# Post-norm layer with streamed softmax maxima: PV bursts one key tile later, casts and row fetches moved, the maxima split and turned step by step

## Time and profile before

| | us |
|---|---|
| median of 3 runs (1063.1 to 1064.48) | 1063.52 |
| the profiled execution | 1064.13 |
| its span | 1062.3 |
| PE busy | 1026.5 (97%) |
| DVE busy | 809.5 (76%) |
| ACT busy | 665.1 (63%) |
| POOL busy | 266.2 (25%) |

### The profile page before, as it was taken

One profiled execution on the slowest core, in us unless ns is written; L12 is line 12 of the kernel. 1 busy time (PEld: TensorE's weight loads), 2 busy tenths in 40 slices (PEclk: granted clock), 3 DMA queues, 4 the chain that ended last, 5 costly groups with the idle time before them and its releaser, 6 DMA issues.

```text
span 1062.3 us, 15699 instructions
## 1 busy us (share of the span) xinstructions
PE 1026.5 (97%) x5858; PEld 536.8 (51%) x5858; DVE 809.5 (76%) x1199; ACT 665.1 (63%) x1346; POOL 266.2 (25%) x227
## 2 busy tenths in 40 slices
PE   8999999999999999999999999999999999999996
PEld 3643344433443433443444443333337888888885
DVE  4899978899779799779988899999803475662535
ACT  2368877788778788778766678888863431222221
POOL 2751030141335422246200042844100000000002
PEclk9999999999999999999999999999999999999999
DMA  5274417243142512344140446531217510402011
GB/s 200 80 196 126 106 35 213 52 97 78 52 115 75 105 56 54 82 108 105 34 78 12 116 120 150 124 121 37 93 68 193 166 40 9 111 28 52 1 39 42
DMA packets 64432, 94.87 MB, mean 89 GB/s; under 512 B 37536, under 2 KB 37920, under 8 KB 62272
## 3 DMA queue, kind: packets, MB, share of 16 engines
q1 hardware_dynamic: 63776, 93.10, 33.2%
q10 hardware_dynamic: 576, 0.72, 0.2%
HBM read 53.95 MB, written 27.00 MB: 76 GB/s over the span
## 4 chain that ended last, share of the span: by engine, by line
PE 80%; DVE 10%; ACT 6%; issue 2%; DMA 1%; SPq 0%; POOL 0%; DVEq 0%; POOLq 0%
PE PS L448 21%; PE PV L467 20%; PE PSA L537 15%; PE PS L554 5%; PE PSA L426 5%; DVE nmx L964 5%; PE PS L365 4%; ACT Bn L756 3%; PE PS L493 2%; PE PSA L493 2%; DVE nmx L960 2%; DVE nmx L957 2%; ACT Bn L765 2%; PE PV L554 2%; PE PSA L365 1%
## 5 line engine op out<-in xcount | busy, mean ns | idle before, releaser
L756 ACT ACTIVATE Bn<-PS 128x512 f32<-128x512 f32 x1146 | 548.8, 559 | 125.0 <-PE PS L448 111.1
L448 PE MATMUL PS<-Qt,Kt 50*128 50x512 f32 x1146 | 391.7, 434 | 20.0 <-ACT Bn L756 18.7
L426 PE MATMUL PSA<-Kt,Qt 48*128 48x512 f32 x1024 | 390.0, 459 | 2.2 <-DVE Kt L936 0.8
L964 DVE TENSOR_REDUCE nmx<-PSA 128x1 f32<-128x1024 f32 x256 | 312.2, 1219 | 61.0 <-PE PSA L426 59.8
L448 PEld LDWEIGHTS PS<-Qt,Kt 50*128 50x128 f32 x1146 | 184.4, 184 | 323.6 <-ACT Bn L756 312.7
L467 PE MATMUL PV<-Bn 128*32 128x512 f32 x2048 | 272.8, 605 | 0.0
L426 PEld LDWEIGHTS PSA<-Kt,Qt 48*128 48x128 f32 x1024 | 174.6, 183 | 21.7 <-DVE nmx L964 6.2
L960 DVE TENSOR_REDUCE nmx<-PSA 128x1 f32<-128x512 f32 x256 | 174.5, 682 | 1.4 <-PE PSA L426 1.1
L957 DVE TENSOR_REDUCE nmx<-PSA 128x1 f32<-128x512 f32 x256 | 174.3, 681 | 0.0
L537 PE MATMUL PSA<-x1Th,wr 128*128 128x512 f32 x344 | 135.0, 393 | 0.8 <-DVE sg L1052 0.5
L537 PE MATMUL PSA<-x1Tl,wr 128*128 128x512 f32 x344 | 134.7, 392 | 0.0
(11 more groups left out here) (166 smaller groups left out, 919.4 us busy)
## 6 DMA issues: line engine op xcount, KB each, us to landing
Qt<-pscr SPq DMA_DIRECT2D x90, 128.0 KB, 4.9
A<-in_wf SPq DMA_DIRECT2D x11, 768.0 KB, 6.3
wr<-A SPq DMA_DIRECT2D x33, 256.0 KB, 2.9
pscr<-A SPq DMA_DIRECT2D x16, 512.0 KB, 3.7
vscr<-Bn SPq DMA_DIRECT2D x32, 256.0 KB, 2.0
Kt<-pscr SPq DMA_DIRECT2D x90, 64.0 KB, 2.3
A<-A SPq DMA_DIRECT2D x16, 256.0 KB, 3.7
Bn<-vscr SPq DMA_DIRECT2D x8, 512.0 KB
```

The source lines that it names most:

```text
L426: op = e.matmul(PSA[:, 2 * s + h, :], Qt[n % 3][p:p + NC_, g % 2, 128 * qt:128 * qt + 128], Kt[n % 3][p:p + NC_, 512 * h:512 * h + 512], s ...
L448: e.matmul(PS2[:, i, cols], Kt[n % 3][rows, 128 * kt:128 * kt + 128], Qt[n % 3][rows, g % 2, 512 * qh + cols.start:512 * qh + cols.stop], ...
L756: e.activation(Pb[c % NP_][:, cols], PS2[:, score_bank[c, p], cols], ACT.Exp, scale=0.25).then_inc(*act_exp.next(piece(c, p)))
L964: e.tensor_reduce(nmx[:, hh % 2, c0:c0 + 1], slot_pair(s), AX.XY, ALU.max, negate=True).then_inc(*dve_max[s].next(k))
```

## The change

- The bursts change places: behind chunk 3 of even units, behind chunk 2 of odd ones. The cut chunk is now c % 8 == 7, chunk 3 of odd units, so the pieced burst is the one of odd units and the plain one that of even units.
- Background moves with its burst: in the same units, but behind chunk 2 and the burst, and before chunk 3. `free_banks`, ScalarE's `evacuate_raw` and VectorE's additions (`first_norm`, `add_values`, `add_rows`, now between the two halves of the second step) follow.
- The casts: h0 from 6 to 7 units behind the projection, h1 from 7 to 9, "out" from 8 to 10. For job 1: units 8, 10 and 11 in place of 7, 9 and 10.
- The rows are fetched in unit 5 in place of 3.
- `turn_max` is taken apart for all query halves but the first and the last: the join stays behind step 15, the rounding stands behind step 0 of the next half, the subtraction behind step 1, the transposition behind step 2. So it ends behind the first step of the units u % 8 == 5.
- `write_max` stands in SP's units u % 8 == 4.

```diff
         rope_end = {(0, 1): (0, "h0"), (0, 2): (0, "h1"), (0, 3): (0, "out"),
-                    (0, 4): (1, "rope"), (0, 7): (1, "h0"), (0, 9): (1, "h1"), (0, 10): (1, "out")}
+                    (0, 4): (1, "rope"), (0, 8): (1, "h0"), (0, 10): (1, "h1"), (0, 11): (1, "out")}
         for at_u, j in project_at.items():
-            u0 = 16 * at_u[0] + at_u[1] + 6
-            rope_end.update({divmod(u0, 16): (j, "h0"), divmod(u0 + 1, 16): (j, "h1"), divmod(u0 + 2, 16): (j, "out")})
+            u0 = 16 * at_u[0] + at_u[1] + 7
+            rope_end.update({divmod(u0, 16): (j, "h0"), divmod(u0 + 2, 16): (j, "h1"), divmod(u0 + 3, 16): (j, "out")})
-        gather_at = {(n, {0: 13, 6: 5}.get(n, 3)): n + 2 for n in range(NG - 2)}
+        gather_at = {(n, {0: 13}.get(n, 5)): n + 2 for n in range(NG - 2)}
+        def apart(hh):
+            return 1 <= hh < 2 * NG - 1
-            return [slice(0, 128), slice(128, 512)] if c % 8 == 3 and c < 4 * SPLIT else [slice(0, 512)]
+            return [slice(0, 128), slice(128, 512)] if c % 8 == 7 and c < 4 * SPLIT else [slice(0, 512)]
         def free_banks(u):
-            last = score_bank[4 * u + 3, len(pieces(4 * u + 3)) - 1]
+            last = score_bank[4 * u + 2, 0]
             return (last + 1) % 3, last
...
-                    if u >= 1 and g == (2, 3)[u % 2]:
+                    if u >= 1 and g == (3, 2)[u % 2]:
                         weigh(u - 1)
-                if at_u in project_at:
-                    for h, i in enumerate(free_banks(u)):
-                        project_half(project_at[at_u], h, i, (0, 1, 2, 3))
...
+                        background(u)
...
                     exponent(u, g)
+                    if g == 2 and at_u in project_at:
+                        for h, i in enumerate(free_banks(u)):
+                            evacuate_raw(project_at[at_u], h, i)
                 if u >= 1:
                     finish(u - 1)
-                if at_u in project_at:
-                    for h, i in enumerate(free_banks(u)):
-                        evacuate_raw(project_at[at_u], h, i)
...
-                if k % 16 == 15:
-                    turn_max(hh)
+                if 1 in halves and k % 16 == 15:
+                    join_max(hh)
+                    if not apart(hh):
+                        high_max(hh)
+                        lower_max(hh)
+                        turn_max(hh)
+                if 1 in halves and k > 16 and k % 16 < 3 and apart(hh - 1):
+                    (high_max, lower_max, turn_max)[k % 16](hh - 1)
...
                 maximum(next(steps))
-                maximum(next(steps))
-                if at_u in norm_at:
-                    first_norm(False, 0, norm_at[at_u])
...
+                k = next(steps)
+                if at_u in norm_at or at_u in out_at or at_u == values_at:
+                    maximum(k, (0,))
...
+                    maximum(k, (1,))
+                else:
+                    maximum(k)
...
-                if steps_done(u) // 16 > steps_done(u - 1) // 16:
+                if u % 8 == 4:
                     write_max(steps_done(u) // 16 - 1)
+                if u == SPLIT - 1:
+                    write_max(2 * NG - 1)
```

More of the change, by code:

```diff
@@ L665, in tensor, with background @@
                     project_half(1, 1, 3, ((0, 1), (2, 3))[k - 2])
+            def background(u):
+                at_u, pair = divmod(u, 16), free_banks(u)
+                if at_u in project_at:
+                    for h, i in enumerate(pair):
+                        project_half(project_at[at_u], h, i, (0, 1, 2, 3))
+                if at_u == values_at:
+                    for t in range(8):
+                        value_rows(1, t, pair[t // 4])
+                if at_u in out_at:
+                    t2 = out_at[at_u]
+                    out_project(False, 0, t2, [bank(i) for i in pair], [bank_free[i] for i in pair])
+                    for j, i in enumerate(pair):
+                        bank_free[i] = dve_y.at((False, 0, 2 * t2 + j))
             for u in range(SPLIT):
@@ L945, in add_values, with maximum @@
                     ALU.add).then_inc(*dve_val.next((b, h)))
-            def maximum(k):
+            def maximum(k, halves=(0, 1)):
                 if k >= len(stream):
@@ L955, in maximum @@
                 if by_halves(k):
[L956 to L961, removed]
+                    for h in halves:
+                        w.wait_ge(*pe_max.at((k, 0) if h == 0 else k))
+                        col = nmx[:, hh % 2, c0 + 16 * (h == 0):c0 + 16 * (h == 0) + 1]
+                        e.tensor_reduce(col, slot_pair(s)[:, h, :], AX.X, ALU.max, negate=True).then_inc(
+                            *dve_max[s].next((k, 0) if h == 0 else k))
                 else:
@@ L965, in maximum, with join_max @@
                         *dve_max[s].next(k))
-                if k % 16 == 15:
-                    turn_max(hh)
-            def turn_max(hh):
+                if 1 in halves and k % 16 == 15:
[6 more added lines that the diff above has]
+                    (high_max, lower_max, turn_max)[k % 16](hh - 1)
+            def join_max(hh):
                 top, rest = nmx[:, hh % 2, 0:16], nmx[:, hh % 2, 16:24]
@@ L973, in turn_max, with high_max @@
                 e.tensor_tensor(top[:, 0:8], top[:, 0:8], rest, ALU.min).then_inc(*dve_ms.next(("join", hh)))
+            def high_max(hh):
                 w.wait_ge(*dve_ms.at(("join", hh)))
@@ L976, in turn_max, with lower_max @@
                     w.wait_ge(*dve_ms.at(("turn", hh - 1)))
-                e.tensor_copy(msp[:, 0:16], top).then_inc(*dve_ms.next(("high", hh)))
+                e.tensor_copy(msp[:, 0:16], nmx[:, hh % 2, 0:16]).then_inc(*dve_ms.next(("high", hh)))
+            def lower_max(hh):
                 w.wait_ge(*dve_ms.at(("high", hh)))
-                e.tensor_tensor(msp[:, 16:32], top, msp[:, 0:16].bitcast(F32), ALU.subtract).then_inc(
+                e.tensor_tensor(msp[:, 16:32], nmx[:, hh % 2, 0:16], msp[:, 0:16].bitcast(F32), ALU.subtract).then_inc(
                     *dve_ms.next(("low", hh)))
+            def turn_max(hh):
                 w.wait_ge(*dve_ms.at(("low", hh)))
@@ L1218, in vector @@
                 maximum(next(steps))
-                maximum(next(steps))
-                if at_u in norm_at:
-                    first_norm(False, 0, norm_at[at_u])
[L1222 to L1226, removed]
+                k = next(steps)
+                if at_u in norm_at or at_u in out_at or at_u == values_at:
+                    maximum(k, (0,))
+                    if at_u in norm_at:
+                        first_norm(False, 0, norm_at[at_u])
+                    if at_u == values_at:
+                        for h, i in enumerate(free_banks(u)):
+                            add_values(1, h, i)
+                    if at_u in out_at:
+                        add_rows(False, 0, out_at[at_u], [bank(i) for i in free_banks(u)])
+                    maximum(k, (1,))
+                else:
+                    maximum(k)
                 if at_u in recip_at:
```

## The result

The changed kernel took **1074.19 us** (median of 4 runs, 1070.33 to 1074.88); the kernel before, run beside it, 1063.37. The ratio is 1.0092 with a 95% interval of 1.0067 to 1.0117: slower, by 10 to 11 us. The forecast was 1055.6. The profiled execution took 1074.88, its span is 1073.1, and its mean granted TensorE clock is 0.982, where before it was 0.998.

The account below looks back on a forecast made before the run. The attention loop was taken as a ring, PE waiting for banks that ACT frees. Gains of -23.7 us and +15.5 for late maxima rows gave -8.2: 1055.6 us, own range 1048 to 1061, 8 in 10 range 1039 to 1065.

Parts of the forecast that it names:

- Part 1: ACT's copy of PV, now behind the plain burst, stops stretching the loop: 0.50 us in each of 30 halves, -15.0 us.
- Part 2: DVE's turn of the maxima, taken apart, gains 0.29 us in each of 19 halves without background: -5.5 us.
- the 0.15 that I let stand: Part of the turn's 0.44 us per half expected to remain, as a later wait on L960.
- the 0.6 to 0.8 of my count: Expected DVE time in us, over two units, for the turn's four small instructions, against 0.9 in one place.
- Part 3: ACT's casts, all in even units now: six projections save 0.51 us each, less 0.35 for job 1, -2.7 us.
- Part 4: Background moved with its burst, ACT resuming with a piece in place of a whole chunk: -0.5 us in all.
- Part 5: Maxima's rows come later; their write queues behind the spread read, so PE waits at six places: +15.5 us.
- The margin of 0.9: Time in us by which the maxima's rows were to arrive before the first scores of unit 8, in undisturbed halves.
- The write was held up: Denies the rival that the maxima's write on SP is not held up, part 5 being 0: 1040 us, chance 0.15.
- DVE did gain: Denies the rival that the turn's four steps gain DVE nothing, part 2 being 0: 1061 us, chance 0.10.
- the copy was hidden: Denies the rival that the copy misses the next burst by 0.25 us, 7.5 in all: 1063 us, chance 0.10.
- The slower one: Rival: rows late at first scores in 24 undisturbed halves too, at 5.5 us write plus read: 1073 us, chance 0.15.

Follow-up runs that it names:

- experiment 10: Kernel before, with turn taken apart, rows fetched in unit 5, reciprocals' read behind the maxima's write, POOL's splits and additions one unit later: 1063.18 us, ratio 0.9997.
- experiment 11: Changed kernel, with spread read one unit later and over 16 rows, second casts and "out" later, POOL's splits and additions one unit later: 1042.80 us, ratio 0.9815.
- experiment 1: Changed kernel, with the reciprocals' spread read issued one unit later, behind the maxima's write and read-back: 1050.22 us, ratio 0.988.
- experiment 5: Changed kernel, with reciprocals written twice to DRAM so the spread read has 16 source rows instead of 8, SP's order kept: 1053.95 us, ratio 0.9902.
- experiment 3: Changed kernel, with 6 to 14 extra matmuls in front of the six late scores to keep PE busy: 1062.58 us, ratio 0.9997.
- experiment 2: Changed kernel, with the turn in one piece behind step 15 and the maxima written in units u % 8 == 3: 1062.71 us, ratio 0.9986.
- experiment 7: Experiment 1's kernel, with the sixth reciprocal's turn moved from (12, 6) to (12, 14): 1051.11 us, ratio 0.9868.
- experiment 8: Experiment 7's kernel, with the second casts 11 units behind the projection instead of 9 and "out" 12 instead of 10: 1047.69 us, ratio 0.9851.

## Why the prediction was wrong

- **Part 1, the copy: right.** Experiments 10 and 11 differ in the bursts, the casts and the DMA edits; in an ordinary half without casts they differ by 20.22 - 19.76 = 0.46, in a background half by 26.36 - 25.89 = 0.47. Over 29 halves this is -13.4 (forecast -15.0).
- **Part 2, the turn: right in kind, undersized.** 20.65 before, 20.22 in experiment 10: 0.43 in each of 17 halves, -7.3 (forecast -5.5). The half then has none of the 0.15 that I let stand: the turn costs DVE some 0.5 us in place of the 0.6 to 0.8 of my count. It gains in 17 halves and not in 19.
- **Part 3, the casts: half of it was never there.** In the halves with background a cast cost 0.5 (26.91 and 26.80 against 26.37), and this went: -1.0. In the four ordinary halves with a cast it cost 0.11 over the turn alone (20.76 against 20.65), and I priced it at 0.51 (the rows give 3.56 - 3.04 = 0.52): the same wait can't be saved twice. -1.4 in all (forecast -2.7).
- **Part 4, background: nothing** beyond the copy (forecast -0.5).
- **Part 5, the stands: right in place, number and size**, 16.06 for 15.5. The margin of 0.9 held in the undisturbed halves, where no stand appeared. That the write's place behind the read is the cause is shown by experiments 1 and 5; on which of the 16 DMA engines the write runs, by none.
- **The step that failed** is part 5's price, which took a stand of PE to cost its own length. The stands did cost their length (16.2 by experiment 3's halves), but around each of the five longer ones TensorE also ran at half clock (0.50), 30.7 of the 34.1 us shown in the windows. Experiment 3 measures the clock at +11.6 between medians; between the profiled executions it is +13.5, of which some 12 go with the stands and some 1.5 with the stretch at 385.8. The term was not in the sum, nor among the rivals.
- **A second term was missing:** DVE's subtraction against POOL. In experiment 3, whose clock stayed up, the five halves with a late subtraction are 0.84, 0.83, 0.83, 0.44 and 0.82 longer than in experiment 11, so it is +3.8. In part 2 I asked what each small step waits for, not what runs beside it on POOL. The subtraction now starts 2.49 us behind the join where it started 0.41 behind it, and so it fell four times under `low_half` and once under an addition.

Sum of the profiled execution, copies alone: -13.4 - 7.3 - 1.4 + 0.4 (what is left over) + 16.1 + 13.5 + 3.8 = +11.7, which is 723.36 - 711.70. The forecast for it was -8.2. Of the 19.9 us between them 13.5 are the clock and 3.8 the collisions.

No rival was right. The write was held up (six stands), DVE did gain, and the copy was hidden. The slower one had the right place (scores of u % 8 == 0) and reached 1073 by lateness in 24 undisturbed halves; there was none in any. That its number is near the result is chance.

Open: what decides whether the clock falls. Over all profiles it fell with each of the eleven stands of 2.03 us or more and not behind the three of 1.64 and 1.93. Of the shorter ones, eight lasted 1.12 to 1.51, and four of these had a fall and four had none. Five falls came 0.8 to 2.2 us after PE had waited for a reduction that was late behind a collision: 385.8 in the changed kernel, 379.1 in experiment 2, 377.2 in experiment 5, and 483.3 and 667.6 in experiment 7. The waits were 0.42, 1.41, 0.43, 0.40 and 0.73 us:

```profile
383.59 0.49 PE L430 MATMUL PSA<-Kt,Qt 48*128 48x512 f32 x1 [0.42 <-DVE nmx L971]
```

The same waits at 164.03 and 331.23 in the changed kernel had none. So the second side effect can bring on the first; that it does is not shown, as no experiment isolates it.

## What to carry to other kernels

When a transfer moves later in a queue, look at what then stands in front of it: the order of two DMAs was worth 24 us here, as much as all forecast gains together. Price a stand of TensorE with the slow matmuls behind it: the five stands of 2.04 to 3.56 us, 14.4 in sum, cost some 12 us again. Where the stand can't be removed, filling it with matmuls was cheaper here than idling. And before a small VectorE instruction is moved, look at GpSimd's row at its new time, not only at VectorE's own.

## What the runs showed of the hardware that I had not expected

- A VectorE subtraction of 128x16 elements takes 0.17 us alone and up to 1.02 beside a GpSimd instruction of 1.29; the join beside the product of 2.38 us took 1.60 and 2.03. The rounding, a cast with one input (msp<-nmx), was caught each of the three times that it met one: 1.22 us in experiment 2, 1.18 in experiment 7, 0.86 in experiment 8. The 32-column transposition, with one input too (mrow<-msp), was not caught in 80 meetings.
- 14 matmuls of 128 columns (28 in the trace) in a stand of 3.39 us kept the granted clock at 1.00; without them it was 0.50 for 6.83 us.
- A 16 KB write behind a 512 KB read took 6.47 us to be seen as landed with the read over 8 rows, 3.62 over 16, and 2.00 ahead of it. The read over 8 rows kept 0.51 of the core's DMA engines at work, over 16 rows 1.00.
